# Two cross-attention layers on one core: the image-token steps of layer 1 placed later among the maxima steps

## What is computed

```python
text_ehs, ip_ehs = enc[:, :-4], enc[:, -4:]            # 371 text rows, 4 image tokens
probs_t  = softmax(q @ k_t.T * scale)                  # text attention
text_out = probs_t @ v_t
attn_scores = q @ k_ip.T * scale                       # 4 scores a head
qsem = l2norm(probs_t @ text_ehs)                      # needs the Gram matrix here
sem  = qsem @ l2norm(ip_ehs).T
probs_ip = softmax(attn_scores + 0.5 * sem) * mask[:, None]
ip_out = probs_ip @ v_ip
out = (text_out + ip_out) @ W_out + b_out + residual
```

## Time and profile before

| | |
|---|---|
| median of 3 runs | 2811.07 us (2806.88 to 2814.4) |
| the profiled execution | 2810.17 us |
| its span, first to last instruction | 2808.4 us |
| PE busy | 2666.7 us, 95% of the span |
| DVE / ACT / POOL busy | 1709.4 (61%) / 1253.6 (45%) / 468.7 (17%) us |
| mean granted TensorE clock | 0.988 of full speed |

### The profile page before, as it was taken

How to read it: one execution, slowest core, us unless ns; L and a number is a source line. 1 busy time by engine, 2 the same in 40 slices (tenths; PEclk the granted TensorE clock), 3 DMA queues, 4 the chain that set the end, 5 groups by cost and what they waited for, 6 DMA issues and landing times.

```text
span 2808.4 us, 61414 instructions
## 1 busy us (share of the span) xinstructions
PE 2666.7 (95%) x25096; PEld 2083.7 (74%) x25096; DVE 1709.4 (61%) x3464; ACT 1253.6 (45%) x2265; POOL 468.7 (17%) x681
## 2 busy tenths in 40 slices
PE   6899999999999999999999999999999999999977
PEld 5677777777777777777777777777777777777755
DVE  3465666765666755666755666655666655667654
ACT  2344444444444444444444444444444444444443
POOL 1111121111121111121111111111111111111100
PEclk8999999999999999999999999999999999999988
DMA  7576546665546765546764556674557665567630
GB/s 196 97 85 87 83 80 83 90 85 84 84 78 84 93 85 81 82 76 90 88 90 79 83 77 86 83 98 76 82 80 88 84 91 80 83 83 85 85 35 7
DMA packets 450078, 236.31 MB, mean 84 GB/s; under 512 B 220459, under 2 KB 449787, under 8 KB 449788
## 3 DMA queue, kind: packets, MB, share of 16 engines
q1 hardware_dynamic: 433958, 209.34, 55.9%
q10 hardware_dynamic: 15840, 23.04, 2.7%
HBM read 166.38 MB, written 64.59 MB: 82 GB/s over the span
## 4 chain that ended last, share of the span: by engine, by line
PE 76%; DVE 13%; SPq 3%; ACT 3%; DMA 3%; issue 2%; POOL 0%; DVEq 0%; ACTq 0%; POOLq 0%
PE R L715 7%; PE ST L672 6%; PE R L569 5%; PE PN L689 5%; PE PN L745 5%; PE R L559 4%; PE R L616 4%; PE PN L732 4%; DVE m L899 4%; PE R L565 3%; PE R L718 3%; PE R L720 3%; PE R L629 3%; PE R L630 3%; PE R L766 2%
## 5 line engine op out<-in xcount | busy, mean ns | idle before, releaser
L1133 ACT ACTIVATE p<-ST 128x1344 f32<-128x1344 f32 x320 | 413.3, 1291 | 155.3 <-PE ST L675 149.5
L715 PE MATMUL R<-pr,Gh 128*128 128x448 f32 (+1 forms) x960 | 369.9, 385 | 28.4 <-DVE acc L801 28.4
L804 DVE SCALAR_TENSOR_TENSOR w<-p,pr 128x1344 f32<-128x1344 f32 x160 | 249.3, 1558 | 227.0 <-ACT pr L1148 227.0
L801 DVE TENSOR_TENSOR rem<-R,kst 128x375 f32<-128x375 f32 (+1 forms) x160 | 87.6, 547 | 485.2 <-ACT kst L1028 485.2
L801 DVE TENSOR_TENSOR w<-R,w 128x448 f32<-128x448 f32 (+1 forms) x480 | 290.7, 622 | 104.0 <-PE R L720 95.5
L629 PE MATMUL R<-wvh,ch 128*128 128x320 f32 (+3 forms) x896 | 302.8, 338 | 11.2 <-DVE cl L801 10.9
L630 PE MATMUL R<-wvh,cl 128*128 128x320 f32 (+3 forms) x896 | 279.6, 312 | 0.0
L672 PEld LDWEIGHTS ST<-Qs,Ks 100*128 100x128 bf16 (+1 forms) x3520 | 189.1, 98 | 88.0 <-issue 32.9
L1194 POOL TENSOR_TENSOR kst<-rem,kst 128x375 bf16<-128x375 f32 (+1 forms) x160 | 146.6, 916 | 618.7 <-ACT kst L1028 319.9
L672 PE MATMUL ST<-Qs,Ks 100*128 100x112 bf16 (+1 forms) x3520 | 228.7, 214 | 15.5 <-DMA Qs<-ms 6.8
L1148 ACT ACTIVATE pr<-ST 128x1344 fp32r<-128x1344 f32 x160 | 205.3, 1283 | 82.2 <-PE R L720 82.2
(11 more groups left out here) (178 smaller groups left out, 5761.7 us busy)
## 6 DMA issues: line engine op xcount, KB each, us to landing
Ks<-k_split SPq DMA_DIRECT2D x384, 140.6 KB, 6.4
k_split<-kst SPq DMA_DIRECT2D x128, 281.2 KB, 3.1
Ks<-k_split SPq DMA_DIRECT2D x384, 93.8 KB, 9.4
Qs<-q_split SPq DMA_DIRECT2D x384, 70.0 KB, 9.2
cT<-in_ctxT ACTq DMA_DIRECT2D x30, 750.0 KB, 4.7
q_split<-qst SPq DMA_DIRECT2D x128, 84.0 KB, 2.0
k_split<-kst SPq DMA_DIRECT2D x64, 140.6 KB, 2.9
xT<-in_xT SPq DMA_DIRECT2D x32, 192.0 KB, 3.2
```

Of the source, the lines that this page charges most:

```text
L715: e.matmul(r[0:nj, 0:QW], Gh[0:ROWS[u], q:q + nj], pr[0:ROWS[u], QW * u:QW * u + QW], start=u == 0, stop=False)
L801: return e.tensor_tensor(to, x, y, op)
L804: return e.scalar_tensor_tensor(out=to, in0=x, scalar=s, in1=y, op0=op0, op1=op1)
L1133: e.activation(p32[i][:].rearrange("p (u q) -> p u q", u=3), st, ACT.Exp).then_inc(p_whole, 1)
```

## The change

One line of `between` is different. The first three pieces of `last` stay after steps 1, 2 and 3; `ip_T` moves from step 5 to 6, `ip_mm` from 7 to 8, `o_T` from 9 to 11, and `o_mm` with `out` from 10 to 12. No instruction is added or removed.

```diff
             count[0] += 1
             if count[0] > 9:
                 take(rows0, 1)
-            if count[0] in (1, 2, 3, 5, 7, 9, 10):
+            if count[0] in (1, 2, 3, 6, 8, 11, 12):
                 take(last, 1)
             if count[0] in (2, 4, 6, 8, 11, 12, 14, 16):
                 take(pieces, 1)
```

## The result

The changed kernel takes 2886.51 us in the median of 5 runs (2883.81 to 2889.55), the kernel before 2811.07 us. The ratio is 1.0259, with a 95% interval of 1.0245 to 1.0273. So it is slower by 75 us by the medians and by 73 by the ratio, where 49 were forecast and 2838 to 2890 was the range. The profiled execution has a span of 2882.0 us against 2808.4, 73.6 us more, and that is what the traces have to account for.

What follows compares the result with a forecast made beforehand. PE, busy 95% of the span, was taken to bound the kernel. The terms, 0.09 + 1.68 - 0.13 = 1.64 us a turn, by 30, gave 49 us and a forecast of 2860 us, range 2838 to 2890.

Steps and rivals of the forecast that it cites:

- The side: Whole kernel: slower by more than the 0.3% bound, chance 0.90.
- the lost cover: In front of step 11: without o_mm there, PE sits idle 1.24 us; o_mm then costs 1.68 us behind step 12.
- the forecast itself: Whole kernel: 2860 us, 1.75% slower, without a fall of the clock; chance 0.64.
- rival A: The clock falls as well: 1.46 us a fall, 2904 if in all 30 turns, 2882 in half; chance 0.22.
- Which turns, and who leads where: Every term counts in 30 turns; VectorE leads from 1041.20 to 1050.00, PE from 1056.50 to 1067.00.
- ip_T: Moved behind step 6, it loses the cover of VectorE's read of step 4 and costs 0.2 us a turn.
- ip_mm: Moved from step 7 to 8: costs nothing, at most 0.3 us if VectorE's gap there were gone.
- o_T and m_T: Without o_T in front of step 10, PE waits 0.29 us longer for m_T, 0.39 in all.
- o_mm and step 11: Step 11 waits 1.24 us, o_mm costs 1.68 us behind step 12; together 1.77 us a turn.
- Queues: On SP, m_split's six DMAs go ahead of out, gaining 0.13 us a turn; other queues cost nothing.
- The sum: 0.09 + 1.68 - 0.13 = 1.64 us a turn, by 30: 49 us; lower bound 2838.
- The clock: Turn 0's clock fell behind the same waits, 1.46 us a fall; left out of the sum, partly in the range.

Runs made afterwards that it cites:

- e1: Kernel before with only ip_T (step 5 to 6) and ip_mm (7 to 8) moved: 2822.13 us, ratio 1.0026.
- e2: Kernel before with only o_T (step 9 to 11) and o_mm with out (10 to 12) moved: 2876.91 us, ratio 1.0220.
- e7: Kernel before with the second value projection behind step 5 instead of 6, ip_T behind 6, out behind 12: 2804.03 us, ratio 0.9960.
- e3: Kernel before with only o_mm and out moved, from step 10 to 12: 2849.58 us, ratio 1.0131.
- e5: Changed kernel with one value projection moved from behind step 11 to behind step 10: 2844.24 us, ratio 1.0104.
- e6: Kernel before with only the output DMA moved, from step 10 to 12, behind the six DMAs of m_split: ratio 0.9994.
- e4: Changed kernel with six unused matmuls added between m_T and step 11 in turns 1 to 30: 2862.48 us, ratio 1.0180.
- e11: Changed kernel with the third value projection moved behind step 9 and o_mm behind step 13: 2819.39 us, ratio 1.0017.
- e8: Kernel before with ip_softmax moved to step 6, ip_T 8, ip_mm 10, o_T 12, o_mm and out 13, third value projection 10: 2825.44 us, ratio 1.0039.
- e10: Kernel before with ip_softmax moved to step 6, ip_T 10, ip_mm 11, o_T 13, o_mm and out 14, third value projection 9: 2833.08 us, ratio 1.0062.
- e12: e10 with one more wait: POOL starts its subtraction for a turn's fourth value projection only after m_neg: 2807.63 us, ratio 0.9982.

## Why the prediction was right, and where it was short

The side was right, and so were the mechanism and the place of the lost cover, which is 47 of the 75 us. The time lies in the range, but the forecast itself was 27 us low, and what came true is not the forecast (chance 0.64) but rival A (0.22), added to its sum. The range holds the result because it took in part of rival A, and the result lies 3.5 us below its upper end. Nothing in the prediction said that the clock would fall in 16 turns rather than in 30 (2904, outside); that part is luck. Term by term:

- **Which turns, and who leads where.** Right: e1 and e2 add up to the whole, with their terms counted in 30 turns, and e7 showed that VectorE leads there, since the wait came back at step 7.
- **ip_T.** 0.2 us taken, 0.22 measured by e1. Step 6 starts when VectorE lets it, and the wait for fus went into the wait for the read (1.34 us).
- **ip_mm.** Costed at nothing. e1 holds it together with ip_T; its 0.22 us a turn leave little room for it. It wasn't run alone.
- **o_T and m_T.** 0.39 us of waiting expected, 0.49 measured.
- **o_mm and step 11.** 1.24 us of waiting expected, 1.15 measured; 1.68 us for o_mm, 1.62 measured. e3, which has this term almost alone, came to 1.18 us a turn against 1.15.
- **Queues.** The scores' wait for Qs<-ms is gone, as expected, but the reason given for it, the six DMAs issued ahead of `out`, is not what removes it: e5 and e6 have that order and keep most of the wait. The 0.13 us can't be told from nothing in e6's time. Nothing else that was passed made itself felt: no wait on a bank or on the value split is in the list.
- **The sum.** 1.64 us a turn, 1.58 measured; 49 us, and e4 with one fall left came to 47. The lower bound was added wrongly: with 0.5 us of o_mm back and the whole DMA gain the sum is 1.64 - 0.5 - 0.1 = 1.04 us a turn, 2842 and not 2838.
- **The clock.** This is the step that failed: "The sum goes without it, the range takes part of it." It was rival A with a chance of 0.22, 1.46 us a fall, and 2882 if the clock falls in half of the turns. It fell in 16 of 30 turns, at 1.58 us each, 25 us, in 15 of them behind step 11. The evidence was in the trace of before: in turn 0, the one turn with the waits that were coming, the clock had fallen. I set that against the waits around ip_T, which are another pair at another place and only 1.07 us together, and counted one direct example for less than it said. A forecast of the sum plus half of rival A's price would have been 2882.

What stays open: what decides, between turns with the same two waits in front of step 11, in which of them the clock falls. Turn 12 and turn 13 above differ in nothing that I could read. The falls aren't scattered, though: from turn 2 to 14 the changed kernel has one in every second turn, and so has e2 from turn 2 to 10. The Trainium skill (page "TensorE: Matmul & The Clock Gate", section on psum-queue depth-cycling) says only that short idle times between groups of matmuls can make the clock go up and down. The trace agrees that they can, and not as a rule for every such time: behind the 1.34 us wait the clock fell in 0 of 30 turns of e1, 1 of the changed kernel and 2 of e11.

## What to carry to other kernels

Before moving a stage in a hand-written order, ask of its old place which wait it covers and of its new place whether anything waits there; a stage that costs nothing in front of a wait costs its full length behind it. If a turn that already has the new pattern is in the trace (a first or last turn often has), read it for all of its effects, the granted clock behind it included, and let it weigh more than the steady turns. And when cover is moved as a remedy, look at what the moved piece covered where it stood (e5, e8).

## What the runs showed of the hardware that was not expected

**Filling idle time can pay.** 180 unused matmuls took some 24 us off the changed kernel (2886.5 to 2862.5, measured in different rounds; 22 us by the ratios 1.0259 and 1.0180), by the clock alone: a turn without a fall is as long with them (86.25 us) as without (86.27).

**A POOL instruction can hold up a VectorE instruction until it ends.** m_neg, 40 elements a row, took 1.13 us in the mean beside POOL's 1.27 us subtraction (e10), and 0.174 us once POOL waited for it (e12). POOL's subtraction, which started 0.13 us sooner in the turn shown, kept its length (1.28 us in e10, 1.27 before). Reductions and copies from PSUM on VectorE beside the same subtraction kept theirs. The Trainium skill (page "SBUF — State Buffer", section on SBUF's two separate sides) says that VectorE in a two-port mode and POOL take one pair of ports in turn, for a whole instruction; e10 and e12 agree, though no run shows in which mode m_neg runs. The kernel before seems to pay a little of it too: the last scaling of ip_softmax (VectorE, line 1014) takes 0.40 us in the median there and ends with POOL's subtraction, and 0.235 us in e12. That wasn't tested by itself. So a stage on POOL that moves can lengthen a small one on VectorE that it shares no semaphore with.
